# A Mamba-2 block with a gated FFN on one core: blocks of 256 tokens in place of 512, in newly written orders

## What is computed

```
xn   = layernorm(u)
z, xBC, dt = xn @ in_proj            # 512, 768 and 8 columns
xBC  = silu(causal_conv4(xBC));  x, B, C = xBC
dt   = softplus(dt + dt_bias);  dA = dt * -exp(A_log)
Y    = selective scan over the sequence, 8 heads of 64, state 128 (in chunks), + D * x
y    = rmsnorm(Y * silu(z)) * norm_weight
x1   = u + layernorm(y @ out_proj)
h    = gelu(layernorm(x1) @ Wg) * (layernorm(x1) @ Wu)      # 2048 hidden columns
out  = x1 + layernorm(h @ Wd)
```

## Time and profile before

| | |
|---|---|
| median of 3 runs | 1010.66 us |
| the profiled execution | 1011.39 us |
| span of its profile, first to last instruction | 1009.7 us |
| PE busy | 922.0 us (91%), 6048 matmuls |
| PE weight loads busy | 808.8 us (80%) |
| DVE busy | 791.9 us (78%) |
| ACT busy | 594.4 us (59%) |
| POOL busy | 338.1 us (33%) |
| chain that ended last | PE 75%, DVE 12%, ACT 6% |

### The profile page before, as it was taken

How to read it: one execution, slowest core, us unless ns; L and a number is a source line. 1 busy time by engine, 2 the same in 40 slices (tenths; PEclk the granted TensorE clock), 3 DMA queues, 4 the chain that set the end, 5 groups by cost and what they waited for, 6 DMA issues and landing times.

```text
span 1009.7 us, 17011 instructions
## 1 busy us (share of the span) xinstructions
PE 922.0 (91%) x6048; PEld 808.8 (80%) x6048; DVE 791.9 (78%) x2079; ACT 594.4 (59%) x1010; POOL 338.1 (33%) x346
## 2 busy tenths in 40 slices
PE   0547797999999999999999999999999999999987
PEld 0436696888888888888888888888888898888887
DVE  4988776898878978798879978798879888887132
ACT  4774957574737666574737665574738565672222
POOL 2022242334242424334252424334152524233232
PEclk9967898999999999999999999999999999999999
DMA  7300000000000000000000000000000000000000
GB/s 230 115 1 11 1 12 1 12 11 2 11 1 32 1 11 1 12 22 1 12 1 32 2 11 1 12 22 1 12 1 32 1 12 1 1 22 1 1 22 11
DMA packets 13828, 17.64 MB, mean 17 GB/s; under 512 B 1712, under 2 KB 10416, under 8 KB 13744
## 3 DMA queue, kind: packets, MB, share of 16 engines
q1 hardware_dynamic: 12880, 16.53, 5.1%
q10 hardware_dynamic: 864, 0.03, 0.1%
HBM read 12.36 MB, written 4.19 MB: 16 GB/s over the span
## 4 chain that ended last, share of the span: by engine, by line
PE 75%; DVE 12%; ACT 6%; issue 4%; DMA 1%; POOL 1%; ACTq 0%; POOLq 0%; DVEq 0%
PE fb L1077 29%; PE mb L1077 15%; PE db L1077 15%; DVE xc L886 6%; PE mb L1187 5%; PE mb L1178 3%; PE mb L1196 3%; PE mb L1170 2%; PE mb L1202 1%; ACT lmat L635 1%; ACT L702 1%; DMA dsk<-in_d_skip 1%; PE mb L1134 1%; DVE raw L877 1%; PE mb L1160 1%
## 5 line engine op out<-in xcount | busy, mean ns | idle before, releaser
L573 POOL TENSOR_TENSOR hl<-hid,hl 128x512 fp32r<-128x512 f32 (+1 forms) x144 | 169.6, 1179 | 412.7 <-ACT hl L709 412.6
L1077 PE MATMUL fb<-x1t,wg 128*128 128x512 f32 (+1 forms) x864 | 215.5, 385 | 5.4 <-DVE x1t L988 5.4
L1077 PE MATMUL db<-wd,hl 128*128 128x256 f32 x1536 | 217.4, 290 | 2.5 <-POOL hl L573 2.5
L1077 PEld LDWEIGHTS db<-wd,hl 128*128 128x128 f32 x1536 | 197.9, 189 | 18.0 <-issue 10.7
L1077 PE MATMUL fb<-x1t,wu 128*128 128x512 f32 (+1 forms) x864 | 206.7, 375 | 3.4 <-ACT hid L702 3.4
L1077 PEld LDWEIGHTS fb<-x1t,wu 128*128 128x128 f32 x864 | 154.0, 193 | 37.0 <-ACT hid L702 5.2
L1077 PEld LDWEIGHTS fb<-x1t,wg 128*128 128x128 f32 x864 | 146.1, 192 | 30.3 <-DVE x1t L988 6.6
L994 DVE TENSOR_TENSOR hid<-fb,hid 128x512 f32<-128x512 f32 (+1 forms) x144 | 90.2, 627 | 75.5 <-PE fb L1077 67.5
L709 ACT ACTIVATE hl<-hid 128x512 fp32r<-128x512 f32 (+1 forms) x144 | 83.4, 580 | 105.3 <-DVE hid L994 78.9
L886 DVE SCALAR_TENSOR_TENSOR xc<-raw,cw,xc 128x256 f32<-128x256 f32 x288 | 132.8, 529 | 10.8 <-ACT xc L655 9.7
L702 ACT ACTIVATE hid<-fb 128x512 f32<-128x512 f32 (+1 forms) x144 | 78.2, 548 | 86.5 <-PE fb L1077 82.7
(11 more groups left out here) (149 smaller groups left out, 1411.7 us busy)
## 6 DMA issues: line engine op xcount, KB each, us to landing
...
```

The source lines that it names most:

```text
L573: pool.tensor_tensor(hl[:, hs, n % 2, 1, :], hid[:, hs, n % 2, :], hl[:, hs, n % 2, 0, :].bitcast(F32), ALU.subtract).then_inc(s["lo"], 1)
L1077: last = pe.matmul(ps, lhs(a, k), rhs(b, k), start=start and n == 0, stop=stop and n == len(todo) - 1, skip_group_check=check)
```

## The change

The block becomes 256 tokens (two tiles): 16 whole blocks, none of them a half. Each iteration runs one Mamba half beside the FFN of 256 tokens. The FFN has eight steps in place of 16. A step takes two 128-column tiles of the hidden columns, so the gate bank still holds 512 columns (2 x 256), but it is filled by 12 matmuls of 256 moving columns instead of 6 of 512. Elementwise instructions keep the shape 128x512. `dn:n` keeps 12 matmuls, and the down product of a block takes one bank, `db[par]`, which alternates by block: `dn:0` waits for `ln4` of the block two before. `x1t`, `dt_` and `ex` are indexed by block parity. The loop of transfers on SP is written out, with the same 16 loads and 16 stores of 256 KB. POOL's `yoff` gets one more wait (`skip`).

```diff
-BLK = 512
-NBLK = BATCH * SEQ // BLK + 1
+BLK = 256
+NBLK = BATCH * SEQ // BLK
+NP = NT // 2
 ORDER = {
     "pe": """
+        ip:2 gu:0< gu:1< z:2 ct:0 dn:0< seg:0 seg:1 gu:2< seg:2 seg:3 gb:0 gu:3< xtr:0 dn:1< yo:0 gu:4< yd:0
+        st:0 dn:2< yt:0 xtr:1 gu:5< dn:3< dn:4< yo:1 out:0 yd:1 st:1 dn:5< gu:6< yt:1 xt:0> gu:7< out:1 ip:0>
+        z:0> z:1> ip:1> dn:6< dn:7< x1t:0 cs:0>""",
     "act": """
+        taps:2 gelu:0< silu:1 split:0< gelu:1< gate:2 silu:2 exps:0 split:1< gelu:2< split:2< gelu:3<
+        decay_matrix:0 decay_matrix:1 decay_matrix:2 split:3< decay_matrix:3 gb_copy:0 gelu:4< square:0
+        yt_split:0 split:4< gelu:5< split:5< square:1 yt_split:1 xn_split:0> gelu:6< split:6< gelu:7< taps:0>
+        dt_bias:0> split:7< gate:0> taps:1> gate:1> x1_split:0 silu:0>""",
     "dve": """
+        inter:0< decays:0 conv:2 sums:0 decay_sums:0 inter:1< decay_sums:1 stats1:0> gb_copy:0 inter:2<
+        decay_sums:2 decay_sums:3 inter:3< xdt:0 decayed_products:0 yoff:0 xn:0> ydiag:0 state:0 inter:4< xdt:1
+        decayed_products:1 inter:5< yt_split:0 yoff:1 ydiag:1 state:1 stats2:0 ln2:0 x1n:0 inter:6< yt_split:1
+        inter:7< xn_split:0> stats2:1 ln2:1 dt_bias:0> conv:0> x1n:1 softplus:0> fin:0< x1_split:0 conv:1>
+        ln4:0<""",
     "pool": """
+        split:0< stats1:0> split:1< xdt:0 yoff:0 split:2< split:3< xdt:1 split:4< yoff:1 split:5< stats2:0 ln2:0
+        split:6< stats2:1 split:7< ln2:1 fin:0<""",
 }
...
             def gu(f, par, n):
                 if n == 0:
-                    pe.wait_ge(s["x1ts"], count("x1ts", f, tiles(f)[-1] // 2))
+                    pe.wait_ge(s["x1ts"], count("x1ts", f, 0))
                 for mat, (name, w) in enumerate((("gate", wg), ("up", wu))):
                     piece_read(f, n, mat)
                     bank_read(f_uses, (name, n), f)
-                    split_matmul(by_half(f_bank[name, n], f), lambda a, k: w[:, a, k, P * n:P * n + P],
-                                 lambda b, k: x1t[:, halves(f), b, k, :], KD).then_inc(s[name], 1)
+                    for e in range(2):
+                        c0 = P * (2 * n + e)
+                        last = split_matmul(f_bank[name, n][:, SUB * e:SUB * e + SUB], lambda a, k: w[:, a, k, c0:c0 + P],
+                                            lambda b, k: x1t[:, par, b, k, :], KD)
+                    last.then_inc(s[name], 1)
...
             def dn(f, par, n):
                 if n == 0:
 
-                    wait_before(pe, "d_read", f - 1, 0)
+                    wait_before(pe, "d_read", f - 2, 0)
```

More of the change, by code:

```diff
@@ L86 @@
-    "dve": """
-        decays:0 inter:0< inter:1< conv:1 inter:2< sums:0 conv:2 decay_sums:0 decay_sums:1 decay_sums:2 inter:3<
-        xdt:0 stats1:1 gb_copy:0 decay_sums:3 decayed_products:0 xn:1 inter:4< yoff:0 ydiag:0 decayed_products:1
-        state:0 inter:5< yt_split:0 inter:6< xdt:1 stats2:0 yoff:1 ln2:0 ydiag:1 xn_split:1 state:1 inter:7<
-        yt_split:1 x1n:0 conv:3 inter:8< stats2:1 dt_bias:1 ln2:1 softplus:1 conv:4 inter:9< decays:1 inter:10<
-        stats1:0> conv:5 sums:1 decay_sums:4 decay_sums:5 decay_sums:6 gb_copy:1 xn:0> inter:11< decay_sums:7
-        decayed_products:2 decayed_products:3 xdt:2 inter:12< yoff:2 inter:13< xn_split:0> ydiag:2 state:2
-        yt_split:2 xdt:3 stats2:2 yoff:3 ln2:2 ydiag:3 state:3 inter:14< x1n:1 yt_split:3 inter:15< x1n:2
-        stats2:3 dt_bias:0> ln2:3 fin:0< x1n:3 x1_split:0 conv:0> x1_split:1 softplus:0> ln4:0<""",
+        ip:2 gu:0< gu:1< z:2 ct:0 dn:0< seg:0 seg:1 gu:2< seg:2 seg:3 gb:0 gu:3< xtr:0 dn:1< yo:0 gu:4< yd:0
@@ L97 @@
-        yoff:1 ln2:0 split:7< split:8< stats2:1 split:9< stats1:0> split:10< split:11< xdt:2 ln2:1 yoff:2
-        split:12< split:13< xdt:3 stats2:2 yoff:3 ln2:2 split:14< split:15< stats2:3 ln2:3 fin:0<""",
+        split:0< stats1:0> split:1< xdt:0 yoff:0 split:2< split:3< xdt:1 split:4< yoff:1 split:5< stats2:0 ln2:0
+        split:6< stats2:1 split:7< ln2:1 fin:0<""",
 }
@@ L147 @@
+        split:1 xdt:0> yoff:0> split:2 split:3 xdt:1> split:4 yoff:1> stats2:0> split:5 ln2:0> split:6 stats2:1>
+        ln2:1> split:7 fin:0 split:0> stats1:0>>> split:1> xdt:0>> yoff:0>> split:2> split:3> xdt:1>> split:4>
+        yoff:1>> split:5> stats2:0>> split:6> ln2:0>> stats2:1>> split:7> ln2:1>> fin:0>""",
 }
@@ L178 @@
 ORDER, FIRST, LAST = parse(ORDER), parse(FIRST), parse(LAST)
-PER_HALF = dict(stats1=1, xn=1, xt=1, xn_split=1, dt_bias=1, softplus=1, cs=1,
-                decays=1, ct=1, sums=1, exps=1,
-                seg=4, decay_sums=4, decay_matrix=4, ip=3, taps=3, conv=3, silu=3, z=3, gate=3, gb=1, gb_copy=1,
-                decayed_products=2, xtr=2, xdt=2, yo=2, yoff=2, yd=2, st=2, state=2, ydiag=2, square=2, yt=2,
-                yt_split=2, out=2, stats2=2, ln2=2, x1n=2, x1t=1, x1_split=1)
-AWAY = dict(before=-1, this=0, next=1, after=2)
+AWAY = dict(before=-1, this=0, next=1, after=2, later=3)
+FIRST_IN_ORDER = 3
 def there(name, k, i):
-    if not isinstance(i, int):
-        return True
-    if name in PER_HALF and (i, k // PER_HALF[name]) in ((0, 0), (NBLK - 1, 1)):
-        return False
     return 0 <= i < NBLK
-def tiles(f):
-    if isinstance(f, int) and f in (0, NBLK - 1):
-        return range(TT // 2, TT) if f == 0 else range(TT // 2)
-    return range(TT)
-def halves(f):
-    return slice(tiles(f)[0] // 2, tiles(f)[-1] // 2 + 1)
-def columns(f):
-    return slice(CH * tiles(f)[0], CH * (tiles(f)[-1] + 1))
 def iteration_steps(engine):
@@ L1018, in ln4 @@
                 dve.wait_ge(s["d_read"], count("d_read", f, 0))
-                for t in tiles(f):
+                for t in range(TT):
                     x = xb[:, par, t, :]
                     last = dve.tensor_scalar(x, x, mr4[:, t:t + 1], None, ALU.subtract)
-                    if t % 2:
-                        last.then_inc(s["outs"], 1)
+                last.then_inc(s["outs"], 1)
             def dq(i, par, q):
@@ L1063, in bank_read @@
                 v, back = u, 0
[L1064 removed]
+                while it - back >= -FIRST_IN_ORDER:
                     v -= 3
```

287 lines of the change are left out of this document (126 added, 161 removed).

## The result

The changed kernel takes 1051.7 us (median, 1050.2 to 1052.8) against 1010.9 for the kernel before: a ratio of 1.0405, 95% interval 1.0389 to 1.0421. It is slower, as forecast, but by 41 us where I forecast 18. The span of its profiled execution is 1048.3 us; the forecast's sum was 1027.9.

A forecast was written before the change was run, and what follows sets the result against it. PE's work was taken to bound the steady part, with DVE close behind. Start-up 95, first interval 66, 14 intervals 822.5 and end 44.4 gave a 1027.9 us span, forecast as 1029 us; 8-in-10 range 1001 to 1052.

The forecast's parts named there:

- The first interval: First `x1t` to the second, with weights still unpacked at a lower clock: 7 us added, 66 us, bounds 60 and 70.
- The 14 others: Intervals from the second `x1t` to the last block's: 14 x 59 - 3.5 = 822.5 us.
- rival C: Idle time at the meeting lowers PE's clock in each iteration: 24 us more, 1053 us; chance 0.12.
- the first `x1t`: Start-up until the first block's `x1t` starts: 95 us, bounds 89 and 102.
- the tail: From the last block's `x1t` to the end of the span: 44.4 us.
- Part 1: Gate and up matmuls cut from 512 to 256 columns: 0.2 us more per block, at most 1.3.
- rival E: Weight loads don't hide behind 256-column matmuls: 180 us more, 1208 us; chance 0.01.
- Part 3: Meeting of two iterations, last `out` to `gu:0`: DVE's chain idles PE 2.7 us per iteration, bounds 1.5 and 4.5.
- Part 4: Rest of an iteration, outside the meeting: PE held 0.3 us more than before, bounds -0.4 and 1.2.
- Part 2: Whole blocks' elementwise steps, ACT's table loads, transfers and POOL's added wait: nothing, bounds -1 to +3 us.

The follow-up runs named there:

- best2_gelu: start_mended with softplus ahead of conv:0, split:7 ahead of dt_bias:0, gate:2 ahead of gelu:1, and tanh Gelu for Silu in three places; 1023.9 us.
- cs_late: The changed kernel with PE's cumulative-sum matmul cs moved behind ip:2; 1054.1 us.
- split7_dve: The changed kernel with step 7's low part subtracted by DVE instead of POOL, and split:7 ahead of dt_bias:0 on ACT, in the loop only; 1045.1 us.
- silu_as_gelu: The changed kernel with tanh Gelu in place of Silu in silu:1, silu:2 and gate:2, no order changed; 1045.9 us.
- before_cut256: The kernel before with only its 512-column gate and up matmuls issued as pairs of 256 columns; 1013.0 us.
- fin_mid: The changed kernel with DVE's fin:0 and ln4:0 moved from the meeting into idle time of the next iteration, and cs behind ip:2; 1043.0 us.
- start_mended: fin_mid with the start-up order written like the steady one at its first two meetings and unpacking steps moved later; 1030.8 us.
- best3: start_mended with softplus ahead of conv:0, split:7 ahead of dt_bias:0, cs ahead of ip:2, and z:2 behind seg:0 on PE; 1030.5 us.

## Why the prediction was right and wrong

**Where it failed.** Two terms of the sum carry the miss in about equal parts. The first interval was put at 66 us and measured 76.75. The 14 others were put at 822.5 and took 834.4; some 2 us of that lie in the second and third, still in the start-up, and the rest in every iteration. There it is the part outside the meeting that failed: the rest of an iteration, from `gu:0` to the next last `out`, was put at 47.3 us (Parts 2 and 4, with ACT's tenth table load at nothing) and measured 48.25, of which 0.9 is PE held up by ACT at `seg:1`.

**Right.** The sign; the kind of loss (a meeting of two iterations twice as often, with less work of PE over it); the chain from `out:1` to `gu:0`, 11.4 us against 11.85 forecast; the names of the waits (`dn:7` for `hl`, `cs` for `da`); PE's granted clock at 1.00 in all iterations, so rival C is out; the first `x1t` and the tail. Part 1 cost 2.0 us against 3 forecast, so rival E is out. The interval, 59.69 against 59.1 in the sum, was nearer than its pieces: the meeting was 0.4 us shorter than forecast and the rest 1.0 longer.

**Part 3, the meeting: its length was right, its parts were not.** Forecast were 9.1 us of PE's own steps and 2.7 us of idle time. PE's own steps I had put together by adding durations; in best2_gelu the same steps, from `ip:0` to `gu:0`, take 10.5 us with no wait over 0.3. The differences lie at `cs` (0.57 us until `ip:2` starts, put at 0.15), `z:0` and `z:1` (1.85 against 1.46) and `ip:2` (1.77 against 1.42). In the kernel after they take 11.4, so its waits cost 0.9 us and not 2.7. `gu:0`, which was to lead them, doesn't wait at all. The forecast of the length did not suffer, because DVE's chain sets it and not PE's steps (cs_late, split7_dve).

**Part 4, the rest of the iteration, failed, and Part 2 with it.** Forecast 0.3 us (at most 1.2) over PE's work; the rest of the iteration came out 1.0 longer than that. I had costed ACT's tenth table load at nothing because ACT is busy 61% in the steady part. That was the mean again: at the head of an iteration it is 89% busy, and `gate:2` behind `gelu:1` and two loads makes `seg:1` wait. That place (from `ct` to `gu:2`, 2.9 us against 2.0) costs 0.9 us, and with three loads fewer and nothing else changed (silu_as_gelu) it takes 2.0 as well. What one load by itself costs no run shows. Set against the kernel before, 1.3 us more remain in each iteration that no experiment removed: best2_gelu has 57.99 us without a named wait over 0.3, the kernel before 56.55, of which the cut explains 0.12. In the traces the starts of 34 matmuls in an iteration of the kernel after lie 150 ns or more behind the one before, 29 in best2_gelu, and 22 for 256 tokens in before_cut256; so part of the time is in short gaps, mostly where a step begins. By step, each start less the usual spacing behind the matmul before it, best2_gelu spends 1.0 us more than before_cut256 at `ip` (0.2 of it is a named wait for ACT's `taps:1`), 0.45 at `dn`, 0.35 in `out`, 0.3 at `z` and 0.2 at `gu`, and about 1.0 less at the transposes, the decays and `yd`. So most of what remains lies in the steps of the meeting, beside its named waits. What makes these gaps isn't shown; that stays open.

So the excess of 3.1 us per 256 tokens over the interval before lies in these places: 0.1 (cut), 0.9 (meeting), 0.9 (ACT at `seg`) and 1.2 to 1.3 (short gaps). I had 0.2, 2.7 and 0.3 over the 55.9 us of PE's work, or 2.5 over the same 56.55.

**The ends: the first interval.** Forecast 66 (60 to 70), measured 76.75. I added half of PE's old idle time to one interval, a guess about work. Most of the miss is not the work: with every unpacking step kept, other places in the written order give 69.1 us and bring the first `x1t` 5.5 us forward. The start-up order was costing 10 to 12 us (fin_mid to start_mended, by the ratios 10.4 and by the medians 12.2), about half of the 22.7 us by which the median missed. The 69.1 is still 3 us over the forecast, and what makes these no run shows.

**The clock.** The prediction named a lower clock in the first interval and gave it no price of its own. It fell there behind each of the four idle times of 2.4 to 2.6 us, so such an idle time cost its own length and again part of the 3 us that follow at 1.2 GHz. It doesn't follow every time: behind the 2.71 us at 124.82 in start_mended it stayed at 1.00.

**What can be given back.** 21 of the 41 us, by order alone (start_mended 1030.8, best3 1030.5). No version beats the kernel before. With three table loads taken out as well (and so another output), best2_gelu is still 12 us behind it.
